# A two-layer recurrent kernel: biases loaded as four rows, and the weights' scaling moved between ticks

## The reference

```python
# layer 0, a plain RNN (512 wide)
next_h = jnp.tanh(prev_h @ WhR + (x_t @ WxR + bR))
y = x + h                      # residual
# layer 1, an LSTM (4 gates of 512, c starts at 0, h at h0)
a = (y_t @ WxL + bL) + prev_h @ WhL
i, f, o = sigmoid(a[:, :H]), sigmoid(a[:, H:2*H]), sigmoid(a[:, 2*H:3*H])
g = tanh(a[:, 3*H:])
next_c = f * prev_c + i * g
next_h = o * jnp.tanh(next_c)
out = y + h                    # residual
```

## Time and profile before

| what | value |
|---|---|
| time, median of 3 | 896.36 us (896.06 to 897.02) |
| the profiled execution's own time | 897.4 us |
| its span | 895.6 us |
| TensorE busy | 862.8 us, 96% of the span |
| VectorE busy | 746.0 us, 83% |
| ScalarE busy | 396.8 us, 44% |
| GpSimd busy | 223.3 us, 25% |
| mean granted clock of TensorE | 0.994 |

### The profile page before, as it was taken

The page is one execution under the profiler, slowest core; times in us unless marked ns, Lnnn a source line. Parts: engine busy times, 40 slices in busy tenths (PEclk is TensorE's granted clock), DMA queues, the critical chain, the costliest instruction groups (busy, mean ns, idle before and its releaser), DMA issues.

```text
span 895.6 us, 42232 instructions
## 1 busy us (share of the span) xinstructions
PE 862.8 (96%) x18572; PEld 506.4 (57%) x18572; DVE 746.0 (83%) x1963; ACT 396.8 (44%) x1062; POOL 223.3 (25%) x503
## 2 busy tenths in 40 slices
PE   4789999999999999999999999999999999999996
PEld 3445655565655556555565555656556556565642
DVE  4568988888888888888888888888888888888874
ACT  2645334444444444444444444444444444444431
POOL 1111122222222222222222222222222222222210
PEclk9999999999999999999999999999999999999999
DMA  9901001111000111100111010011011000000000
GB/s 331 252 2 27 17 12 27 27 27 26 23 18 16 27 26 26 27 15 15 27 27 27 26 27 14 16 27 26 26 27 27 12 6 15 14 15 15 15 14 14
DMA packets 39329, 30.38 MB, mean 34 GB/s; under 512 B 4328, under 2 KB 37864, under 8 KB 37864
## 3 DMA queue, kind: packets, MB, share of 16 engines
q1 hardware_dynamic: 38724, 27.48, 11.0%
q10 hardware_dynamic: 420, 0.20, 0.1%
HBM read 19.27 MB, written 8.39 MB: 31 GB/s over the span
## 4 chain that ended last, share of the span: by engine, by line
PE 86%; DVE 6%; SPq 2%; DMA 2%; issue 2%; ACT 1%; POOL 0%; POOLq 0%; DVEq 0%
PE ps_l L774 36%; PE ps_l L800 31%; PE ps_r L839 8%; PE ps_r L856 8%; PE ps_l L789 2%; DMA wxl_raw<-in_L_cond_Wx 2%; SPq L286 1%; SPq L266 1%; DVE pre_l L605 1%; ACT gates L416 1%; DVE h_lo L640 1%; DVE h_hi L627 1%; PE ps_r L814 1%; PE ps_r L824 1%; ACT tanh_c L423 1%
## 5 line engine op out<-in xcount | busy, mean ns | idle before, releaser
L800 PE MATMUL ps_l<-wxl_hi,whl_raw 128*32 128x512 f16 x3840 | 251.2, 379 | 0.0
L800 PEld LDWEIGHTS ps_l<-wxl_hi,whl_raw 128*32 128x32 f16 x3840 | 104.2, 97 | 103.5 <-issue 5.0
L313 POOL TENSOR_TENSOR xb<-xb,h_l 128x128 f32<-128x128 f32 x128 | 59.1, 462 | 333.6 <-DVE h_l L633 333.6
L774 PE MATMUL ps_l<-whl_hi,hT_hi 128*32 128x512 f16 x2016 | 131.1, 380 | 5.0 <-DVE hT_hi L631 3.1
L336 POOL TENSOR_TENSOR yT<-xT,hT_r 128x128 f32<-128x128 f32 x128 | 58.6, 458 | 295.6 <-DVE hT_r L673 295.6
L774 PE MATMUL ps_l<-whl_lo,hT_hi 128*32 128x512 f16 x2016 | 131.5, 381 | 0.0
L774 PE MATMUL ps_l<-whl_hi,hT_lo 128*32 128x512 f16 x2016 | 131.1, 380 | 0.0
L605 DVE SCALAR_TENSOR_TENSOR pre_l<-ps_l,g_products,bias_l 128x256 f32<-128x256 f32 x240 | 105.1, 479 | 26.1 <-PE ps_l L774 19.5
L800 PE MATMUL ps_l<-wxl_lo,whl_raw 128*32 128x512 f16 x1920 | 125.6, 379 | 0.0
L656 DVE SCALAR_TENSOR_TENSOR pre_r<-ps_r,g_products,xr 64x128 f32<-64x128 f32 x224 | 78.4, 350 | 34.2 <-POOL xr L326 29.3
L428 ACT ACTIVATE h_r<-pre_r 128x128 f32<-128x128 f32 x128 | 39.6, 309 | 143.4 <-DVE pre_r L656 106.6
(11 more groups left out here) (101 smaller groups left out, 1278.1 us busy)
## 6 DMA issues: line engine op xcount, KB each, us to landing
out<-xb SPq DMA_DIRECT2D x128, 64.0 KB, 1.8
xb<-in_x SPq DMA_DIRECT2D x126, 64.0 KB, 2.1
whl_raw<-in_L_cond_Wh SPq DMA_DIRECT2D x4, 1024.0 KB, 13.2
wxl_raw<-in_L_cond_Wx SPq DMA_DIRECT2D x4, 1024.0 KB, 17.9
wxr_raw<-in_L_cond_Wx SPq DMA_DIRECT2D x1, 1024.0 KB, 5.5
whr_raw<-in_L_cond_Wh SPq DMA_DIRECT2D x1, 1024.0 KB, 7.5
bias_l<-in_L_cond_b SPq DMA_DIRECT2D x4, 64.0 KB, 14.7
xb<-in_x ACTq DMA_DIRECT2D x2, 64.0 KB, 2.4
```

Source lines behind the costliest of these rows:

```text
L313: nc.gpsimd.tensor_tensor(xb[g % NX][:, t, :], xb[g % NX][:, t, :], h_l[s % 2][:, :], ALU.add).then_inc(out_done, 1)
L774: last = nc.tensor.matmul(ps_l[s % 2][quarter(j), :], (hT_hi, hT_lo)[h_part][:, k, :], gate_slice(whl[w_part][k], j), start=False, stop=(h ...
L800: last = nc.tensor.matmul(ps_l[s % 2][quarter(j), :], y16[y_part][g % 2][:, k, t * B:(t + 1) * B], gate_slice(wxl[w_part][k], j), start=(y ...
```

## The change

Three things are edited.

1. The biases. Instead of one transfer of `bias_r` and four of `bias_l`, 64 KB each, spread over the partitions by the source's address pattern, a transfer of 2 KB on SyncE's queue brings four rows of 128 for the RNN, and one of 8 KB on ScalarE's queue (ahead of h0) four rows of 512 for the LSTM. VectorE makes a 4x128 pattern of zeros and ones; two TensorE products spread the rows into `ps_l[0]` and `ps_l[1]`, and ScalarE copies them out. The four rows and the pattern stand in buffers that are not yet in use.
2. SyncE's order. x group 1 comes behind chunk 2 of WhL (before: behind chunk 1), x group 2 ahead of all chunks of WxL (before: behind chunk 0 of it); the bias transfers between chunks 1 and 2 of WxL are gone.
3. The ticks. WhL's exchange: the turn at the end of TensorE's tick 3, the spread in tick 4 right behind `recurrent_r`, the scale ahead of `rnn_turn` of tick 4. WxL's exchange is one tick later (tick 8). Bounds: WhL 2 moves from tick 1 to 2, WhL 3 from 2 to 3, WxL 0 from 6 to 3, WxL 1 stays at 6 alone. High halves: WhL 3 moves from tick 5 to 6; WxL 0 from 8 to 9, WxL 2 from 9 to 10, WxL 3 from 10 to 11. Low halves: WhL 2 moves from tick 7 to 6, so that tick 7 keeps WhL 3 alone; WxL 0, 1 and 2 move from ticks 9, 10, 11 to 10, 11, 12, so that tick 12 has WxL 2 and 3. `y_scale` of group 0 moves from tick 6 to 5, `rnn_weight_scale` from tick 3 to 2.

```diff
@@ tables
-        SCALE_AT = {OF_H: 4, OF_X: 7}
+        SCALE_AT = {OF_H: 4, OF_X: 8}
-        W_LOW_AT = {5: (OF_H, 0), 6: (OF_H, 1), 9: (OF_X, 0), 10: (OF_X, 1), 11: (OF_X, 2), 12: (OF_X, 3)}
-        W_LOW_LAST_AT = 7
+        W_LOW_FIRST_AT = {5: [(OF_H, 0)]}
+        W_LOW_AT = {6: [(OF_H, 1), (OF_H, 2)], 7: [(OF_H, 3)], 10: [(OF_X, 0)], 11: [(OF_X, 1)], 12: [(OF_X, 2), (OF_X, 3)]}
-        W_BOUND_AT = {0: [(OF_H, 0)], 1: [(OF_H, 2)], 2: [(OF_H, 3)], 6: [(OF_X, 0), (OF_X, 1)], 7: [(OF_X, 2), (OF_X, 3)]}
-        W_HIGH_AT = {4: [(OF_H, 0)], 5: [(OF_H, 1), (OF_H, 2), (OF_H, 3)], 8: [(OF_X, 0)], 9: [(OF_X, 1), (OF_X, 2)], 10: [(OF_X, 3)]}
+        W_BOUND_AT = {0: [(OF_H, 0)], 2: [(OF_H, 2)], 3: [(OF_H, 3), (OF_X, 0)], 6: [(OF_X, 1)], 7: [(OF_X, 2), (OF_X, 3)]}
+        W_HIGH_AT = {4: [(OF_H, 0)], 5: [(OF_H, 1), (OF_H, 2)], 6: [(OF_H, 3)], 9: [(OF_X, 0), (OF_X, 1)], 10: [(OF_X, 2)], 11: [(OF_X, 3)]}
-        Y_SCALE_AT = {6: 0, 8: 1}
+        Y_SCALE_AT = {5: 0, 8: 1}
@@ SyncE
-            sp.dma_start(bias_r[:, :], bass.AP(tensor=bR.tensor, offset=0, ap=[[P, J], [0, B], [1, P]])).then_inc(s_bias_r, DMA)
+            sp.dma_start(bias_rows_r, bR.rearrange("(j u) -> j u", j=J)).then_inc(s_bias_r, DMA)
             load_chunk(whl_raw[1][:, :], WhL, 1, s_whl[1])
+            load_chunk(whl_raw[2][:, :], WhL, 2, s_whl[2])
             load_x(sp, 1)
-            load_chunk(whl_raw[2][:, :], WhL, 2, s_whl[2])
             load_chunk(whl_raw[3][:, :], WhL, 3, s_whl[3])
-            load_chunk(wxl_raw[0][:, :], WxL, 0, s_wxl[0])
             load_x(sp, 2)
-            load_chunk(wxl_raw[1][:, :], WxL, 1, s_wxl[1])
-            for j in range(J):
-                sp.dma_start(bias_l[quarter(j), :].rearrange("p (g u) -> p g u", g=G),
-                             bass.AP(tensor=bL.tensor, offset=j * P, ap=[[0, B], [H, G], [1, P]])).then_inc(s_bias_l, DMA)
-            load_chunk(wxl_raw[2][:, :], WxL, 2, s_wxl[2])
-            load_chunk(wxl_raw[3][:, :], WxL, 3, s_wxl[3])
+            for k in range(J):
+                load_chunk(wxl_raw[k][:, :], WxL, k, s_wxl[k])
@@ ScalarE
+            act.dma_start(bias_rows_l.rearrange("j (g u) -> j g u", g=G),
+                          bL.rearrange("(g j u) -> j g u", g=G, j=J)).then_inc(s_bias_l, DMA)
+            act.wait_ge(bias_mm, 2)
+            nc.scalar.activation(bias_r[:, :], ps_l[0][:, 0:P], ACT.Copy).then_inc(bias_done, 1)
+            nc.scalar.activation(bias_l[:, :], ps_l[1][:, :], ACT.Copy).then_inc(bias_done, 1)
@@ VectorE
+            dve.wait_ge(ident_done, 1)
+            nc.vector.tensor_copy(spread_j.rearrange("p (j b) -> p j b", j=J),
+                                  ident[0:J, 0:J].unsqueeze(2).broadcast_to([J, J, B])).then_inc(spread_j_done, 1)
@@ TensorE
+            pe.wait_ge(spread_j_done, 1)
+            pe.wait_ge(s_bias_r, DMA)
+            nc.tensor.matmul(ps_l[0][:, 0:P], spread_j, bias_rows_r, start=True, stop=True).then_inc(bias_mm, 1)
+            pe.wait_ge(s_bias_l, DMA)
+            nc.tensor.matmul(ps_l[1][:, :], spread_j, bias_rows_l, start=True, stop=True).then_inc(bias_mm, 1)
             product_r(0)
...
+                if k + 1 == SCALE_AT[OF_H]:
+                    pe.wait_ge(w_peaked[OF_H], J)
+                    pe.wait_ge(r_step, 1)
+                    turn_peaks(EXCHANGE[OF_H], slice(0, J))
```

More of the change, by code:

```diff
@@ L115, in rnn_lstm_kernel @@
         R_PEAK = 8 + NG
+        bias_rows_l, bias_rows_r, spread_j = pre_l[0:J, :], pre_r[0:J, :], gates[0:J, 0:P]
         y16 = [[whl_raw[3][:, (2 * part + i) * 2 * P:(2 * part + i + 1) * 2 * P].bitcast(F16).rearrange("p (k m) -> p k m", k=J)
@@ L136, in rnn_lstm_kernel @@
         c_zero = sem("c_zeroed")
+        spread_j_done = sem("spread_j_done")
+        bias_mm = sem("bias_product")
+        bias_done = sem("bias_spread")
         h0_turned = sem("h0_turned")
@@ L434, in _ @@
                     cell_tanh(k - LAG)
+                    for of, chunk in W_HIGH_AT.get(k, []):
+                        weight_high(of, chunk)
                     for of, chunk in W_BOUND_AT.get(k, []):
@@ L438, in _ @@
                         rnn_weight_high(R_HIGH_AT[k])
-                    if k >= SCALE_AT[OF_X] + 2:
-                        for of, chunk in W_HIGH_AT.get(k, []):
-                            weight_high(of, chunk)
                 if R0 <= k < T:
@@ L453, in _ @@
                     y_scale(Y_SCALE_AT[k])
-                if k < SCALE_AT[OF_X] + 2:
+                if k < LAG:
                     for of, chunk in W_HIGH_AT.get(k, []):
                         weight_high(of, chunk)
-                if k < LAG:
                     for of, chunk in W_BOUND_AT.get(k, []):
@@ L600, in cell @@
                 if s == 0:
-                    dve.wait_ge(s_bias_l, DMA * J)
+                    dve.wait_ge(bias_done, 2)
                 dve.wait_ge(lstm_mm, s + 1)
@@ L646, in rnn_add @@
                 if r == 0:
-                    dve.wait_ge(s_bias_r, DMA)
+                    dve.wait_ge(bias_done, 1)
                 dve.wait_ge(rnn_mm, r + 1)
@@ L682, in _ @@
                     rnn_add(k)
-                    if k in W_LOW_AT:
-                        weight_low(*W_LOW_AT[k])
+                    for of, chunk in W_LOW_FIRST_AT.get(k, []):
+                        weight_low(of, chunk)
+                    if k == SCALE_AT[OF_H]:
+                        weight_scale(OF_H)
                     rnn_turn(k)
@@ L687, in _ @@
                         spread(EXCHANGE_R, 2)
+                    if k == R_SCALE_AT + 2:
+                        rnn_weight_scale()
                     if k in W_MAX_AT:
                         weight_max(*W_MAX_AT[k])
-                    if k == SCALE_AT[OF_H]:
-                        weight_scale(OF_H)
                     if k in TURN_X_AT:
@@ L694, in _ @@
                     if k == SCALE_AT[OF_H] - 1:
-                        rnn_weight_scale()
                         spread(EXCHANGE[OF_H], J)
@@ L705, in _ @@
                     x_scale(BATCH_AT.index(k - 1))
[L706 to L712, removed]
+                if k == SCALE_AT[OF_X]:
+                    spread(EXCHANGE[OF_X], J)
+                if LAG <= k:
+                    for of, chunk in W_LOW_AT.get(k, []):
+                        weight_low(of, chunk)
                 if k in R_LOW_AT:
@@ L729, in _ @@
                 if k == SCALE_AT[OF_X]:
-                    spread(EXCHANGE[OF_X], J)
+                    weight_scale(OF_X)
                 if k in BATCH_AT:
@@ L740, in step_0_recurrent @@
                 pe.wait_ge(h0_turned, 1)
+                pe.wait_ge(bias_done, 2)
                 for k in chunks:
@@ L885, in _ @@
                     recurrent_r(k)
[L886 to L891, removed]
+                if k == SCALE_AT[OF_X]:
+                    pe.wait_ge(w_peaked[OF_X], J)
+                    pe.wait_ge(w_step[OF_H], 1)
+                    turn_peaks(EXCHANGE[OF_X], slice(J, 2 * J))
                 if k in BATCH_AT:
@@ L900, in _ @@
                     turn_peaks(exchange_x(i), slice(X_PEAK + first, X_PEAK + first + count))
+                if k == SCALE_AT[OF_H]:
+                    spread_peaks(EXCHANGE[OF_H], J)
                 if k < LAG:
@@ L907, in _ @@
                     spread_peaks(EXCHANGE_R, 2)
-                if k == SCALE_AT[OF_H]:
-                    spread_peaks(EXCHANGE[OF_H], J)
                 if k in STEP_0_AT:
                     step_0_recurrent(STEP_0_AT[k])
+                if k + 1 == SCALE_AT[OF_H]:
+                    pe.wait_ge(w_peaked[OF_H], J)
+                    pe.wait_ge(r_step, 1)
+                    turn_peaks(EXCHANGE[OF_H], slice(0, J))
                 if k == LAG - 1:
@@ L922, in _ @@
                 if k == SCALE_AT[OF_X]:
-                    pe.wait_ge(w_peaked[OF_X], J)
-                    pe.wait_ge(w_step[OF_H], 1)
-                    turn_peaks(EXCHANGE[OF_X], slice(J, 2 * J))
+                    spread_peaks(EXCHANGE[OF_X], J)
                 if k in BATCH_AT:
```

## The result

| kernel | median | lowest to highest | runs |
|---|---|---|---|
| before | 896.48 us | 894.09 to 901.02 | 20 |
| changed | 898.53 us | 897.62 to 898.82 | 20 |

The ratio is 1.0018, 95% interval 1.001 to 1.0027: slower by about 2 us, where a gain of some 4 us was forecast. The profiled execution has a span of 896.9 us against 895.6, 1.3 more. The kernel before scatters over 7 us, the changed one over 1.2.

What follows compares the result with a forecast made beforehand. TensorE, busy 96%, was held by three waits: the last weight landing, tick 7 and tick 12. Terms -2.6 - 2.3 - 1.7 + 1.7 = -4.9 us took the profiled 897.4 to 892.5; median forecast 892.3, 8-in-10 range 890.2 to 894.9.

Steps and rivals of the forecast that it cites:

- the new bias path: At the start: bias products and copies, and one more issue delaying h0 by 0.4 to 1.5 us, cost nothing, being hidden.
- A: Load: fewer, cheaper bias transfers land WxL 3 at 37.6 instead of 40.2, gaining 2.6 us, bounds 1.4 to 3.7.
- The RNN ticks 0 to 5: Start: ScalarE is free by 39.2, gates start at 39.3, so these ticks are just covered when WxL 3 lands.
- B: Tick 7: one low half instead of two shrinks TensorE's wait from 3.0 to 0.7 us, gaining 2.3 us.
- D: Clock behind tick 7's wait: product at 2.7 instead of 4.46 us, gaining 1.7 us, bounds 0 and 1.8.
- The rival of a slow stretch at WxL 3: Slow clock in the gap ahead of WxL 3 or at TensorE's tick 13 wait: +1.7 us, 894.0; chance 0.12.
- C: Tick 12: VectorE's second WxL low half delays the chain, a loss of 1.7 us, bounds 0.0 and 2.3.
- ScalarE's wait for WxL 0: Tick 3: late WxL 0 delays step 0's gates; slower by 0.2% if it lands from 36.9 us; chance 0.03.
- Tick 12 costs nothing: Rival: the second low half in tick 12 loses no time, median 890.6 us; chance 0.10.
- tick 6 is overfull: Rival: tick 6's 0.1 us cover is missed, VectorE's lateness reaches tick 7, median 894.6 us; chance 0.05.

Runs made afterwards that it cites:

- experiment 3: Changed kernel, bias rows still first, with h0 loaded in four transfers of 32 partitions each instead of one; 891.04 us, ratio 0.9938 to before.
- experiment 2: Kernel before plus one unused 8 KB transfer ahead of h0's on ScalarE's queue; 899.46 us, ratio 1.0023 to before.
- experiment 9: Kernel before with bias_r's 64 KB transfer issued behind the two RNN matrices instead of ahead; 898.11 us, ratio 1.0002 to before.
- experiment 11: Changed kernel with SyncE waiting for h0's landing ahead of the first 1 MB transfer; 894.30 us, ratio 0.9958 to before.
- experiment 1: Changed kernel with h0's transfer issued ahead of the LSTM's bias rows on ScalarE's queue; 895.61 us.
- experiment 8: Changed kernel's bias path and load order, h0 in quarters, every tick's work as in the kernel before; 891.77 us, ratio 0.9938 to before.
- experiment 5: Kernel before with only the low half of WhL 2 moved from tick 7 to 6; 895.31 us, ratio 0.9971 to before.
- experiment 6: Kernel before with h0's transfer issued first on ScalarE's queue, ahead of x's two quarters; 899.34 us, ratio 1.0014 to before.
- Experiment 4: On top of experiment 1, WxL's low halves one each at ticks 9, 10, 11, 12; 894.19 us.

## Why the prediction was wrong, by its steps

**The step that failed** is the sentence on the new bias path: "One more issue on ScalarE's queue delays h0 by an issue (0.4 to 1.5 us in rows 3 to 6) ... so it is hidden too." I priced the issue and not the large transfers that h0 then had to share the engines with. The issue cost 0.64 us; the arrival moved by 12.7 us, from 5.61 to 18.35, and the end of step 0 by 7.8 (experiment 3). Experiments 2, 9 and 11 show the cause: delay h0's issue alone and it is late (2); start the large transfers earlier alone and it is late (9); hold them back and the same transfer takes 2.8 us (11). Experiment 3 adds that the shape of the transfer counts: in quarters it comes at 10.57. What decides is not simply which issue comes first. With a lead over WxR's issue of 0.71 us h0 was turned at 5.61, with 0.35 at 12.91 (experiment 1), with 0.10 at 17.60 (2), with -0.05 at 11.29 (9) and with -0.28 at 18.35; the two latest are those with the bias rows ahead of it. Why nothing of it moves from 2.32 to 6.6 us in the changed kernel is not shown.

The Trainium skill ("DMA: Bandwidth & Descriptors", why a DMA increments its semaphore by 16 and not by 1) says that a transfer is spread over the largest number of engines, 16 at most, that divides the outermost dimension of both its sides; the source of h0 has 4 there, so 128 pieces go to 4 engines, 32 to each. No view here names an engine, but the groups of about four packets agree with it, and so do the quarters, whose outermost dimension is 32. The same page (queues, rings and completion order) has each engine take turns between the queues it has work for, with typically 9 to 17 descriptors (single pieces) a turn. If the small pieces are on 4 engines, the 76 packets from 8 to 14 us are 76 / 4 / 6 = 3.2 a microsecond on each, against 344 / 16 / 6 = 3.6 of the other queue. The trace agrees with turns, but not with their length: small pieces that come four at a time, evenly, fit turns of one piece. By that estimate h0's 32 pieces an engine cost 33 turns of 0.33 us, 10.8 us. I had looked at the rule on the outermost dimension, and set it aside for the 10 KB of the bias rows, rightly as they stand. The 64 KB behind them had the same shape, and I did not look.

**A** was right in kind and too small: WxL 3 at 36.2, a gain of 4.0 us, above my bound of 3.7. The gain ahead of WxL 2 was 3.5, where I had 2.6, and WxL 3 behind it took 3.7 us (36.2 - 32.5) instead of the 4.2 that I had left as they were; which of the removed small transfers is worth how much is not shown. In experiment 8 it is in the time by itself: TensorE's product starts 3.7 us earlier. The changed kernel could not use it, since the RNN's ticks were not done.

**The RNN ticks 0 to 5.** My "just covered" holds in experiment 3, where step 0's product ends at 36.99, 0.3 us behind WxL 3's landing at 35.6 and the 1.07 us of the last chunk's product. In the changed kernel these ticks started 12.7 us late and were made up to a delay of 7.8 at the end of step 0.

**B** was right: TensorE's wait is 0.81 us, and step 2 starts 59.38 - 44.78 = 14.6 us behind step 0, before 58.19 - 41.32 = 16.9; 2.3 us as summed. Experiment 5 shows it alone: 2.1 us in the time, 2.3 in the profile's gap.

**D** appears in the profile (2.77 us for the 48 products, before 4.46), but experiment 8 has nearly the same wait with the clock at full speed behind it, and so has experiment 2. In experiment 9 the clock fell both there and at WxL 3, in experiment 6 only at WxL 3. So D is no fixed part of that wait, and that it fits the profiles' difference in full was luck. The rival of a slow stretch at WxL 3 names something that these two profiles have and the changed kernel's has not.

**C** was right: from step 2's start to step 10's the changed kernel takes 123.15 - 59.38 = 63.8 us, the one before 63.7, of which 1.7 were the slow clock; C = 1.8. Experiment 4 gives 1.6 back (spans 894.1 and 892.5). TensorE's marked waits add up to 1.9 us (1.32 and 0.56) and not to the 2.4 that I wrote.

**The sum with the failed step mended.** Span: A 4.3 at the end of step 0 (41.32 - 36.99), B 2.3, D 1.7, less C 1.8: 6.5, and 895.6 - 6.5 = 889.1, experiment 3's span. (A is taken from this very execution, so only the rest is tested.) With h0's 7.8 added back it is 896.9, the changed kernel's.

**The rivals.** None was it. The only one that made the kernel slower put it down to ScalarE's wait for WxL 0 in tick 3; WxL 0 landed at 27.8, far from its 36.9. What made the kernel slower was a transfer that I had judged by its own length and not by its neighbours'. "Tick 12 costs nothing" and "tick 6 is overfull" are refuted by experiments 4 and 5.

**Open.** Why the kernel before scatters over 6 to 7 us. Experiment 9, where h0 is late too, has the same scatter, as has experiment 6; the kernels with the new loads scatter by 1 to 3 us. Two things go with it. One is the clock: of the 69 timed runs of the kernel before beside the experiments, the six with a mean granted clock of 0.997 have a median of 895.0 us, the four with 0.990 one of 899.7; in between the times overlap. The other is the landing of WxL 3 with the old loads: 39.2 us in experiment 5, 40.2 before, 41.7 in experiment 9, 42.7 in experiment 6. The two together account for the profiled spans. Experiment 6: 2.5 us of landing, 2.7 of slow clock at WxL 3, less the 1.7 at step 2, make 3.5, and its span is 899.1 - 895.6 = 3.5 longer. Experiment 9: 1.5 of landing and 1.7 of slow clock at WxL 3, with the same slow stretch at step 2 as before, make 3.2, as measured. What makes the landing and the clock differ from one execution to the next is not shown.

## What to carry to other kernels

A transfer whose issue is moved by half a microsecond can arrive ten later if it loses its lead over a stream of large ones: when an edit touches a queue near the start of a backlog, list for every transfer behind it which large transfers it now competes with, and how many engines its outermost dimension gives it. Small loads that the first product needs belong well ahead of the first large one (here 0.7 us of lead was enough and 0.35 was not), or the large one has to wait for them (experiment 11), or they are spread over more engines (experiment 3). And a gain of several microseconds can be complete in the trace and absent from the time: experiment 3 only split one transfer in four to bring out 7.5 us that the change already held.

## What the runs showed of the hardware

- 64 KB in 128 pieces with an outermost dimension of 4: 2.8 us from issue to landing with no large transfer beside it (experiment 11), 16.0 us beside a stream of 1 MB transfers on the other queue (changed kernel); in four transfers with an outermost dimension of 32, 5.3 to 6.9 us each (experiment 3).
- In those 16.0 us nothing of it moved for the first 4.3; then 132 packets came about four at a time, every 0.33 us, while the other queue kept its pace (3.6 packets of mostly 8 KB a microsecond on each of 16 engines).
- 8 KB of the same shape: used 2.8 us behind its issue when it was first on its queue (1.69 and 4.50, changed kernel), 11.5 us when it stood behind h0's 64 KB (2.85 and 14.31, experiment 1).
- The same gap of 3.1 us in TensorE's work, with one short product in it, was followed by 3.4 us at a granted clock of 0.50 (1.2 GHz) in one execution (before) and by none in another (experiment 8).
